# Attention and mixture of experts on one core: the reciprocal of the softmax sums moved in part from VectorE to ScalarE, and the masked scores kept in PSUM

## The chip, the cores and the metric

The kernel runs on 1 core of one Trainium2 chip. The metric is the device time of one execution in microseconds (us), lower is better. The engines are PE (TensorE, matmuls), DVE (VectorE), ACT (ScalarE), POOL (GpSimd) and SP (SyncE, DMA issue).

## The reference, cut to what matters

```python
# x: (4, 1024, 256); 16 heads of 64
proj = x @ W_in.T + b_in
q, k = _rope(q, sin, cos), _rope(k, sin, cos)
att = einsum('bhqd,bhkd->bhqk', q, k) / 8
att = where(causal, att, -inf)
att = softmax(att, axis=-1)             # exp(att - max) / sum
y = einsum('bhqk,bhkd->bhqd', att, v)
x = layernorm(x + y.reshape(...) @ W_out.T + b_out)
...
x = layernorm(x + ffn(x))               # 16 experts, the best 3 of each token
```

The change touches the attention alone: the division by the softmax sum, and the masking of the scores from which the row maxima come.

## The kernel before, in words

Attention is worked in 32 steps (`STEPS`): 4 batches times 8 pairs of heads (`PAIRS`), each step on all 1024 tokens. Every engine runs its own instruction stream, written out by hand as a list of events for one turn (`PE_ORDER`, `ACT_ORDER`, `DVE_ORDER`, `POOL_ORDER`, `SP_ORDER`, lines 37 to 47). `turns` walks these lists for `it` from -2 to 32; a `+` behind an event works on the next step, `++` on the one after it, `-` on the one before. An engine never leaves the order of its list, so an instruction that waits holds back all behind it. The streams are tied by semaphores only. `PE_LAST` and `ACT_LAST` (lines 116, 117) stand in for the lists in the last turn.

The events that matter here, with the line where each is made:

- A (PE, L599) fills `a_ps` with scores of queries against keys, one bank for each of the two heads (.0 and .1), in 12 units of up to 512 columns. M (DVE) takes the negated row maximum: a plain reduction where no entry is masked (L921), and where the unit is on the diagonal a fused instruction (L917 and 918) that subtracts the causal mask, writes the result into `masked` (bf16, SBUF), and gives the minimum; the written tile is never read. A of the next unit waits for M of this one (L637), as they share the bank.
- B (PE, L606 and L607) fills `b_ps` with the transposed scores minus the maxima, E (ACT, L798) takes the exponential into `prob`. B of the next unit and head waits for E of this one (L650): B6.1 waits for E5.1, B7.1 for E6.1, B4.1 for E3.1.
- V (PE, L688) multiplies `prob` with the values into `y_ps`; N (ACT, L835) copies `y_ps` to `yT`.
- The sums over the keys are added up in `acc` for one half of the queries by DVE (k, L955 to L960), for the other by POOL (K, L534); D0 and D1 (PE, L698) sum over the partitions with a matrix of ones into `t_ps`.
- d0 and d1 (ACT, L839) copy `t_ps` to `inv`. R0 to R7 (DVE, L966) take the reciprocal of `inv` in place, 128 columns at a time, four for each half; G0 and G1 (DVE, L970) multiply `yT` by it.
- O0 to O3 (PE, L713) project `yT` with W_out into `t_ps`, o0 to o3 (DVE, L980) add that to the rows of `x1b`.
- `t_ps` is one bank that D, O and X (the turning of the maxima, L708) share, so PE waits before each for the one before it (`wait_misc`, L611 to L622): O1, which comes behind D0, waits for `d_taken` from d0.
- r (DVE, L937) and a, l (POOL, L507 and L512), h (ACT, L811) make the rotated queries and keys and their high and low halves for the step after the next; T (POOL, L520) zeroes the masked corner of `prob`; y (ACT, L830), z (DVE, L892) and u (POOL) are the first layer norm, in some turns only; v (ACT, L821) evicts the values.

Around the change the order on PE is `V3 B5.1 B6.0 A5.1+ O1- A6.0+ B6.1 B7.0 X0+ A6.1+ B7.1`, that on ACT is `d0 h2++ E5.1 E6.0 N0 E6.1`. Half a turn before, PE has `D1- V8- V9- V10- V11- B3.1 B4.0 A4+ B4.1 F1++`, and ACT has `d1- h0++ N1- E3.1 E4.0 E4.1`.

Of the kernel before, what the change touches and what calls it, by code (L numbers as in the profile page):

```python
# [7 lines left out]
ALU = mybir.AluOpType  # L8
ACT = mybir.ActivationFunctionType
AX_X = mybir.AxisListType.X  # L10
F32 = mybir.dt.float32
# [20 lines left out]
def parse(text):  # L32

    return [(w.rstrip("+-"), w.count("+") - w.count("-")) for w in text.split()]
# [5 lines left out]
A10.1+ A11.0+ F3++ A11.1+""")  # L40
ACT_ORDER = parse("""E0.0 E0.1 E1.0 E1.1 E2.0 w1 E2.1 E3.0 d1- h0++ N1- E3.1 E4.0 E4.1 y0 h1++ E5.0 d0 h2++ E5.1 E6.0 N0 E6.1 y1 E7.0
w0+ E8.0 E7.1 h3++ E8.1 y2 E9.0 E9.1 y3 E10.0 v2++ E10.1 E11.0 E11.1 v3++""")
DVE_ORDER = parse("""M11.1 M0.0+ C0 M0.1+ M1.0+ M1.1+ M2.0+ k0 M2.1+ M3.0+ k1 k2 r0++ M3.1+ R4- r1++ R5- M4.1+ k3 M4.0+ R6- R7-
M5.0+ r2++ G1- r3++ z0 M5.1+ o1- M6.0+ R0 M6.1+ R1 M7.0+ R2 R3 G0 z1 M7.1+ o2- M8.0+ M8.1+ M9.0+ o3- M9.1+ M10.0+
o0 M10.1+ M11.0+""")
# [70 lines left out]
PE_LAST = [(e, -1) for e in "V8 V9 V10 V11 t0 D1 t1 g0 O1 g1 O2 l0 O3".split()]  # L116
ACT_LAST = [(e, -1) for e in "N1 c0 d1 c1 e0 f0".split()]
GATED = 4
# [15 lines left out]
def attention_phase(nc, A, dram, shared):  # L134
# [4 lines left out]
    with ExitStack() as ctx:  # L139
# [3 lines left out]
        def sem(name):  # L143
# [18 lines left out]
        acc = sb("acc", [P, 2, 2, 512], F32)  # L162
        inv = sb("inv", [P, 2, 512], F32)
        cos = sb("cos_sb", [P, T], F32)
        sin = sb("sin_sb", [P, T], F32)
        yT = sb("yT", [P, 2, 512], F32)
        ident, bout = shared["ident"], shared["bout"]
        causal = sb("causal", [P, 512], F32)
        masked = sb("masked", [P, 2, 512], BF16)
        ones = sb("ones64", [P, 64], F32)  # L170
# [16 lines left out]
                 "p_fill pv_done y_taken max_all turned d_fill d_taken o_fill o_done rope_read v_taken "  # L187
                 "diag_full cut added hi_done lo_done sum_d sum_p inv_all g_done x_st x_back "
                 "bout_sum bout_all biased ln_stat ln_chain ln_ready normed ln_mean "
# [12 lines left out]
        exp_done = [sem(f"exp_done{h}") for h in range(2)]  # L202
        inv_done = [sem(f"inv_done{c}") for c in range(2)]
        m_row = [sem(f"m_row{c}") for c in range(2)]
# [544 lines left out]
        def _(act):  # L749
# [11 lines left out]
            def finish_high_halves():  # L761
                high_halves(EARLY, NW + NX)
                for i, (r, c) in enumerate(WO_UNITS):
# [3 lines left out]
                                         ACT.Copy).then_inc(m["wo_ev"], 1)  # L767

            high_halves(0, EARLY)

            def turn(it, phase, order):
                for e, ahead in order:
# [59 lines left out]
                    elif kind == "N":  # L832
                        act.wait_ge(m["pv_done"], UNITS * n + (4 if q == 0 else UNITS))
                        wait_for(act, m["o_fill"], 4 * (n - 1) + 2 * q + 2, n - 1)
                        nc.scalar.activation(yT[:, q, :], y_ps[:], ACT.Copy).then_inc(m["y_taken"], 1)  # L835
                    elif kind == "d":
                        act.wait_ge(m["d_fill"], 2 * n + q + 1)
                        wait_for(act, m["g_done"], 2 * (n - 1) + q + 1, n - 1)
                        nc.scalar.activation(inv[:, q, :], t_ps[:], ACT.Copy).then_inc(m["d_taken"], 1)  # L839
                    elif kind == "c":  # L840
                        act.wait_ge(m["x_turned"], q + 1)
                        act.wait_ge(m["added"], 4 * STEPS)
                        nc.scalar.activation(rot[:, q, :], g_ps[:, q, :], ACT.Copy).then_inc(m["x_taken"], 1)
                    elif kind == "e":
                        act.wait_ge(m["lt_fill"], 2)
                        act.wait_ge(m["rope_read"], 4 * STEPS)
                        nc.scalar.activation(cos[0:E_, 0:512], a_ps[0:E_, 0, :], ACT.Copy).then_inc(m["lt_taken"], 1)
                    elif kind == "f":
                        act.wait_ge(m["lt_turned"], 1)
                        nc.scalar.activation(shared["early_lg"][:].rearrange("p t e -> p (t e)"), a_ps[:, 1, 0:GATED * E_],  # L850
                                             ACT.Copy).then_inc(shared["early_in"], 1)
# [4 lines left out]
        def _(dve):  # L856
# [42 lines left out]
            def turn(it, phase, order):  # L899
                for e, ahead in order:  # L900
# [10 lines left out]
                    elif kind == "M":  # L911
# [4 lines left out]
                        if diagonal:  # L916
                            nc.vector.tensor_tensor_reduce(  # L917
                                masked[:, h, 0:w], a_ps[:, h, 0:w], causal[:, 512 - w:512], -1.0, -MASKED, ALU.add,
                                ALU.min, out).then_inc(a_max[h], 1)
# [42 lines left out]
                    elif kind == "R":  # L962
                        c, i = q // 4, q % 4
                        dve.wait_ge(m["d_taken"], 2 * n + c + 1)
                        part = inv[:, c, i * P:(i + 1) * P]
                        nc.vector.reciprocal(part, part).then_inc(inv_done[c], 1)  # L966
                    elif kind == "G":
                        dve.wait_ge(inv_done[q], 4 * (n + 1))
                        dve.wait_ge(m["y_taken"], 2 * n + q + 1)
                        nc.vector.tensor_tensor(yT[:, q, :], yT[:, q, :], inv[:, q, :], ALU.mult)\  # L970
                            .then_inc(m["g_done"], 1)
                    elif kind == "o":
# [6 lines left out]
                        rows = x1[:, first:first + 2, :].rearrange("p t d -> p (t d)")  # L979
                        nc.vector.tensor_tensor(rows, t_ps[:], rows, ALU.add).then_inc(m["o_done"], 1)  # L980

# [859 lines left out]
```

## Time and profile before

| | us |
|---|---|
| three timed runs | 1835.0, 1840.57, 1841.21 |
| median | 1840.57 |
| span of the profiled execution | 1831.6 |

The profiled execution has no time of its own beside its span in what is shown; the span runs from the first to the last instruction, and the median of the timed runs is 9.0 us above it. The attention fills the span from about 90 to 1280 us, then come routing, the experts and the last layer norm. In the views below a row of the timeline gives the start, the length, the engine, the line, the instruction and its tiles, and in brackets the idle time of that engine before it with what ended it. PEld is the loading of weights into PE, which runs ahead of the matmuls.

### The profile page before, as it was taken

The numbers are of one execution on the slowest core, as the hardware profiler recorded it, in microseconds if no ns is written. First come the engines' busy times: TensorE is split into PE (matmuls) and PEld (weight loads), VectorE is DVE, ScalarE is ACT, GpSimd is POOL, SyncE is SP. The second block draws the span as 40 slices with busy tenths as digits, with TensorE's granted clock in tenths as the row PEclk, the third lists the DMA queues.
The fourth block names the chain that finished last, engine by engine and source line by source line (L and its number), as shares of the span: only waits on it lengthen the run. The fifth ranks groups of instructions, "written<-read, shape, count | busy, mean of one in ns | idle before, by whom it ended". The sixth has DMA issues, their size and how long they took to land. (4 is left out here: it accounts for less than half of the span.)

```text
span 1831.6 us, 34098 instructions
## 1 busy us (share of the span) xinstructions
PE 1689.9 (92%) x9515; PEld 1265.2 (69%) x9516; DVE 1381.3 (75%) x3236; ACT 728.9 (40%) x1551; POOL 1233.2 (67%) x1064
## 2 busy tenths in 40 slices
PE   4699999999999999999999999998659999999990
PEld 4566667666766677666766676664249999999980
DVE  3578888888888888988888898885775566556654
ACT  2244444444444544444444444543352222222222
POOL 2266787677877776788777777764017777777764
PEclk8699999999999999999999999999759999999995
DMA  9975566655755776556776564531954444444448
GB/s 310 336 217 151 162 170 201 171 173 157 190 150 177 229 219 190 157 164 199 211 218 187 173 185 139 162 104 50 369 158 72 73 74 72 71 73 74 71 65 278
DMA packets 185571, 302.37 MB, mean 165 GB/s; under 512 B 23632, under 2 KB 82896, under 8 KB 185312
## 3 DMA queue, kind: packets, MB, share of 16 engines
q1 hardware_dynamic: 161872, 269.20, 49.5%
q0 software_dynamic: 21504, 30.29, 10.4%
q10 hardware_dynamic: 2064, 1.31, 0.3%
q8 instruction: 60, 0.98, 0.2%
q14 instruction: 71, 0.58, 0.1%
HBM read 188.81 MB, written 111.67 MB: 164 GB/s over the span
## 5 line engine op out<-in xcount | busy, mean ns | idle before, releaser
L798 ACT ACTIVATE prob<-b_ps 128x512 f32<-128x512 f32 (+3 forms) x768 | 354.4, 488 | 357.0 <-PE b_ps L607 255.8
L534 POOL TENSOR_TENSOR acc<-acc,prob 128x1024 f32<-128x1024 f32 (+1 forms) x192 | 353.0, 1839 | 6.4 <-POOL acc L534 3.7
L606 PE MATMUL b_ps<-q,k 128*128 128x512 f32 (+3 forms) x768 | 295.8, 389 | 4.8 <-ACT prob L798 3.5
L507 POOL TENSOR_TENSOR roped<-rot 128x512 f32<-128x512 f32 x128 | 174.7, 1365 | 164.1 <-DVE rot L937 163.1
L599 PE MATMUL a_ps<-k,q 128*128 128x512 f32 (+3 forms) x768 | 266.2, 383 | 16.9 <-DMA k<-scratch_hilo 6.7
L688 PE MATMUL y_ps<-prob,v_sb 128*64 128x512 f32 (+3 forms) x1536 | 272.9, 490 | 0.1
L917 DVE CUSTOM_DVE_ANT_0 masked<-a_ps,causal 128x128 bf16<-128x128 f32 (+3 forms) x512 | 237.2, 478 | 42.7 <-PE a_ps L599 35.2
L607 PE MATMUL b_ps<-q,k 65*128 65x512 f32 (+3 forms) x768 | 264.2, 348 | 0.0
L1487 POOL DMA_INDIRECT scratch_sum<-y,dst_i x112 | 186.5, 1665 | 96.2 <-ACT y L1559 90.4
L966 DVE RECIPROCAL inv<-inv 128x128 f32<-128x128 f32 x256 | 232.2, 929 | 7.7 <-ACT inv L839 5.3
L512 POOL TENSOR_TENSOR lo<-roped,hi 128x512 fp32r<-128x512 f32 x128 | 177.0, 1383 | 81.2 <-ACT hi L811 81.2
L688 PEld LDWEIGHTS y_ps<-prob,v_sb 128*64 128x64 f32 x1536 | 104.3, 137 | 179.1 <-issue 174.3
L1513 PEld LDWEIGHTS h_ps<-mxT,w_now 128*128 128x128 f32 x1792 | 219.4, 193 | 5.7
L1513 PE MATMUL h_ps<-mxT,w_now 128*128 128x128 f32 x1792 | 219.8, 276 | 0.0
L1522 PE MATMUL yo_ps<-w,hT 128*128 x896 | 211.8, 379 | 0.0
L591 PE MATMUL g_ps<-xT,w_sb 128*128 128x512 f32 x768 | 194.0, 403 | 7.4 <-DVE rot L937 4.5
L921 DVE TENSOR_REDUCE max_b<-a_ps 128x1 f32<-128x512 f32 x256 | 171.7, 672 | 36.2 <-PE a_ps L599 33.1
L606 PEld LDWEIGHTS b_ps<-q,k 128*128 128x128 f32 x768 | 145.0, 189 | 73.9 <-issue 42.1
L599 PEld LDWEIGHTS a_ps<-k,q 128*128 128x128 f32 x768 | 142.8, 191 | 61.9 <-DVE max_b L921 12.8
L1472 POOL DMA_INDIRECT xin<-scratch_xn,src_i x112 | 111.5, 996 | 109.1 <-POOLq L1007 75.3
L591 PEld LDWEIGHTS g_ps<-xT,w_sb 128*128 128x128 f32 x768 | 148.0, 196 | 39.5 <-DVE rot L937 5.5
L1522 PEld LDWEIGHTS yo_ps<-w,hT 128*128 128x128 f32 x896 | 161.6, 190 | 17.4
(258 smaller groups left out, 2393.6 us busy)
## 6 DMA issues: line engine op xcount, KB each, us to landing
q<-scratch_hilo SPq DMA_DIRECT2D x192, 256.0 KB, 4.6
k<-scratch_hilo SPq DMA_DIRECT2D x192, 256.0 KB, 5.2
scratch_hilo<-hi SPq DMA_DIRECT2D x64, 512.0 KB, 4.0
scratch_hilo<-lo SPq DMA_DIRECT2D x64, 512.0 KB, 4.7
w_sb<-scratch_wsplit SPq DMA_DIRECT2D x32, 512.0 KB, 3.7
w<-in_L_ffn_W_dram SPq DMA_DIRECT2D x32, 512.0 KB, 10.1
wv_sb<-scratch_wsplit SPq DMA_DIRECT2D x16, 512.0 KB, 6.2
xT<-scratch_xsplit SPq DMA_DIRECT2D x6, 1024.0 KB, 6.6
```

What stands on the lines that cost most here:

```text
L534: nc.gpsimd.tensor_tensor(sums, old, probs(q), ALU.add).then_inc(m["sum_p"], 1)
L591: ins = nc.tensor.matmul(out, left, right, start=(a, b, k) == PRODUCTS[0], stop=(a, b, k) == PRODUCTS[-1], skip_group_check=True)
L599: nc.tensor.matmul(out, q1[s][:, h, blk * P:(blk + 1) * P], k1[s][:, h, k0:k0 + w], start=True, stop=True, skip_group_check=True).then_inc ...
L606: nc.tensor.matmul(out, k1[s][:, h, js], q1[s][:, h, qs], start=True, stop=False, skip_group_check=True)
L607: ins = nc.tensor.matmul(out, k2[s][0:65, h, js], q2[s][0:65, half, h, 512 - w:512], start=False, stop=True, skip_group_check=True)
L688: ins = nc.tensor.matmul(y_ps[64 * h:64 * h + 64, 512 - w:512], v_sb[:, pairs, j, s, 64 * h:64 * h + 64], probs(q)[:, h, :], start=(j == 0 ...
L798: nc.scalar.activation(probs(q)[:, h, :], b_ps[:, h, 0:w], ACT.Exp).then_inc(exp_done[h], 1)
L917: nc.vector.tensor_tensor_reduce(masked[:, h, 0:w], a_ps[:, h, 0:w], causal[:, 512 - w:512], -1.0, -MASKED, ALU.add, ALU.min, out).then_in ...
L966: nc.vector.reciprocal(part, part).then_inc(inv_done[c], 1)
L1487: pool.indirect_dma_start(out=dram[f"sum{t % SUMS}"], out_offset=bass.IndirectOffsetOnAxis(ap=dst_i[:, t:t + 1], axis=0), in_=y[:, t % 2, ...
L1513: ins = nc.tensor.matmul(h_ps[:, s, c * P:(c + 1) * P], w1_now[:, s, k, c * P:(c + 1) * P], xT[:, s, k * P:(k + 1) * P], start=(k == 0), s ...
L1522: ins = nc.tensor.matmul(yo_ps[:, s, 0:D], hT[:, s, c * P:(c + 1) * P], w2[:, bass.ds(e, 1), c, :].rearrange("p a d -> p (a d)"), start=(c ...
```

## The change

For each half of the queries, ACT now takes three steps where it took one: it copies the sums to a new tile `total`, writes their natural logarithm into `inv`, and, in a new event x, replaces `inv` by exp(-inv), a first guess g of 1/s. DVE makes it exact by one Newton step with the sign turned: `total` becomes s*g, and `inv` becomes (s*g - 2)*g. The two instructions are R0 and R1 for half 0, R2 and R3 for half 1, each over 512 columns; the eight reciprocals are gone. As the result is negated, o now subtracts `t_ps` from the rows. Before the attention a table set of ACT that has both functions is loaded by name. The masked scores are written back to `a_ps` in f32 instead of to `masked` in bf16, and that tile is gone.

```diff
--- before.py
+++ after.py
@@ -38,10 +38,10 @@
 V11- B3.1 B4.0 A4+ B4.1 F1++ A5.0+ B5.0 V0 V1 V2 D0 V3 B5.1 B6.0 A5.1+ O1- A6.0+ B6.1 B7.0 X0+ A6.1+ B7.1
 A7.0+ B8.0 V4 V5 V6 V7 B8.1 A7.1+ B9.0 O2- B9.1 B10.0 A8.0+ F2++ A8.1+ B10.1 A9.0+ O3- B11 A9.1+ A10.0+ O0
 A10.1+ A11.0+ F3++ A11.1+""")
-ACT_ORDER = parse("""E0.0 E0.1 E1.0 E1.1 E2.0 w1 E2.1 E3.0 d1- h0++ N1- E3.1 E4.0 E4.1 y0 h1++ E5.0 d0 h2++ E5.1 E6.0 N0 E6.1 y1 E7.0
+ACT_ORDER = parse("""E0.0 E0.1 E1.0 E1.1 E2.0 w1 E2.1 E3.0 d1- h0++ x1- N1- E3.1 E4.0 E4.1 y0 h1++ E5.0 d0 h2++ x0 E5.1 E6.0 N0 E6.1 y1 E7.0
 w0+ E8.0 E7.1 h3++ E8.1 y2 E9.0 E9.1 y3 E10.0 v2++ E10.1 E11.0 E11.1 v3++""")
-DVE_ORDER = parse("""M11.1 M0.0+ C0 M0.1+ M1.0+ M1.1+ M2.0+ k0 M2.1+ M3.0+ k1 k2 r0++ M3.1+ R4- r1++ R5- M4.1+ k3 M4.0+ R6- R7-
-M5.0+ r2++ G1- r3++ z0 M5.1+ o1- M6.0+ R0 M6.1+ R1 M7.0+ R2 R3 G0 z1 M7.1+ o2- M8.0+ M8.1+ M9.0+ o3- M9.1+ M10.0+
+DVE_ORDER = parse("""M11.1 M0.0+ C0 M0.1+ M1.0+ M1.1+ M2.0+ k0 M2.1+ M3.0+ k1 k2 r0++ M3.1+ r1++ R2- M4.1+ k3 M4.0+ R3-
+M5.0+ r2++ G1- r3++ z0 M5.1+ o1- M6.0+ M6.1+ R0 M7.0+ R1 G0 z1 M7.1+ o2- M8.0+ M8.1+ M9.0+ o3- M9.1+ M10.0+
 o0 M10.1+ M11.0+""")
 POOL_ORDER = parse("""K11- u0 T0 u1 T1 u2 T2 u3 a0++ l0++ T3 a1++ l1++ p0 a2++ l2++ K5 a3++ K6 l3++ K7 T8 T9 K8 T10 K9 T11 K10""")
 SP_ORDER = parse("""L1+ S3+ L0++ W0++ S0++ W1++ S1++ S2++""")
@@ -114,7 +114,7 @@
 ZEROS_FROM, ZERO_PIECES = 12, 11
 ZERO_TILES = (TILES + 1) // ZERO_PIECES
 PE_LAST = [(e, -1) for e in "V8 V9 V10 V11 t0 D1 t1 g0 O1 g1 O2 l0 O3".split()]
-ACT_LAST = [(e, -1) for e in "N1 c0 d1 c1 e0 f0".split()]
+ACT_LAST = [(e, -1) for e in "N1 c0 d1 x1 c1 e0 f0".split()]
 GATED = 4
 
 
@@ -161,12 +161,12 @@
         prob = sb("prob", [P, P_SIZE], F32)
         acc = sb("acc", [P, 2, 2, 512], F32)
         inv = sb("inv", [P, 2, 512], F32)
+        total = sb("total", [P, 512], F32)
         cos = sb("cos_sb", [P, T], F32)
         sin = sb("sin_sb", [P, T], F32)
         yT = sb("yT", [P, 2, 512], F32)
         ident, bout = shared["ident"], shared["bout"]
         causal = sb("causal", [P, 512], F32)
-        masked = sb("masked", [P, 2, 512], BF16)
         ones = sb("ones64", [P, 64], F32)
         bias = sb("bias", [P, 3, PAIRS], F32)
         max_a = sb("max_a", [P, 2, 2, 4], F32)
@@ -185,7 +185,8 @@
 
         names = ("vo_done zeroed wv_ld wsp consts ones_row w_in wv_in tab_in bias_in wo_in setup_tr setup_hi setup_lo wo_ev "
                  "p_fill pv_done y_taken max_all turned d_fill d_taken o_fill o_done rope_read v_taken "
-                 "diag_full cut added hi_done lo_done sum_d sum_p inv_all g_done x_st x_back "
+                 "diag_full cut added hi_done lo_done sum_d sum_p g_done x_st x_back "
+                 "guessed scaled refined "
                  "bout_sum bout_all biased ln_stat ln_chain ln_ready normed ln_mean "
                  "x_turned x_taken lt_fill lt_taken lt_turned").split()
         m = {k: sem(k) for k in names}
@@ -200,7 +201,6 @@
         a_max = [sem(f"a_max{h}") for h in range(2)]
         b_fill = [sem(f"b_fill{h}") for h in range(2)]
         exp_done = [sem(f"exp_done{h}") for h in range(2)]
-        inv_done = [sem(f"inv_done{c}") for c in range(2)]
         m_row = [sem(f"m_row{c}") for c in range(2)]
         m_ld = [sem(f"m_ld{c}") for c in range(2)]
 
@@ -766,6 +766,7 @@
                                          setup_bank(NW + NX + i).rearrange("p (j c) -> p j c", j=4),
                                          ACT.Copy).then_inc(m["wo_ev"], 1)
 
+            nc.scalar.preload_act_table_set("natural_log_exp_and_others")
             high_halves(0, EARLY)
 
             def turn(it, phase, order):
@@ -836,7 +837,13 @@
                     elif kind == "d":
                         act.wait_ge(m["d_fill"], 2 * n + q + 1)
                         wait_for(act, m["g_done"], 2 * (n - 1) + q + 1, n - 1)
-                        nc.scalar.activation(inv[:, q, :], t_ps[:], ACT.Copy).then_inc(m["d_taken"], 1)
+                        wait_for(act, m["refined"], 2 * n + q, 2 * n + q - 1)
+                        nc.scalar.activation(total[:], t_ps[:], ACT.Copy)
+                        nc.scalar.activation(inv[:, q, :], t_ps[:], ACT.Ln).then_inc(m["d_taken"], 1)
+                    elif kind == "x":
+
+                        act.wait_ge(m["d_taken"], 2 * n + q + 1)
+                        nc.scalar.activation(inv[:, q, :], inv[:, q, :], ACT.Exp, scale=-1.0).then_inc(m["guessed"], 1)
                     elif kind == "c":
                         act.wait_ge(m["x_turned"], q + 1)
                         act.wait_ge(m["added"], 4 * STEPS)
@@ -915,7 +922,7 @@
                         out = max_a[:, s, h, blk:blk + 1] if blk < 4 else max_b[:, s, k0 // 512, h, blk - 4:blk - 3]
                         if diagonal:
                             nc.vector.tensor_tensor_reduce(
-                                masked[:, h, 0:w], a_ps[:, h, 0:w], causal[:, 512 - w:512], -1.0, -MASKED, ALU.add,
+                                a_ps[:, h, 0:w], a_ps[:, h, 0:w], causal[:, 512 - w:512], -1.0, -MASKED, ALU.add,
                                 ALU.min, out).then_inc(a_max[h], 1)
                         else:
                             nc.vector.tensor_reduce(out, a_ps[:, h, 0:w], AX_X, ALU.max, negate=True)\
@@ -960,12 +967,17 @@
                             ins = nc.vector.tensor_tensor(sums, sums, probs(q), ALU.add)
                         ins.then_inc(m["sum_d"], 1)
                     elif kind == "R":
-                        c, i = q // 4, q % 4
-                        dve.wait_ge(m["d_taken"], 2 * n + c + 1)
-                        part = inv[:, c, i * P:(i + 1) * P]
-                        nc.vector.reciprocal(part, part).then_inc(inv_done[c], 1)
+                        c = q // 2
+                        if q % 2 == 0:
+                            dve.wait_ge(m["guessed"], 2 * n + c + 1)
+                            nc.vector.tensor_tensor(total[:], total[:], inv[:, c, :], ALU.mult)\
+                                .then_inc(m["scaled"], 1)
+                        else:
+                            dve.wait_ge(m["scaled"], 2 * n + c + 1)
+                            nc.vector.scalar_tensor_tensor(out=inv[:, c, :], in0=total[:], scalar=-2.0, in1=inv[:, c, :],
+                                                           op0=ALU.add, op1=ALU.mult).then_inc(m["refined"], 1)
                     elif kind == "G":
-                        dve.wait_ge(inv_done[q], 4 * (n + 1))
+                        dve.wait_ge(m["refined"], 2 * n + q + 1)
                         dve.wait_ge(m["y_taken"], 2 * n + q + 1)
                         nc.vector.tensor_tensor(yT[:, q, :], yT[:, q, :], inv[:, q, :], ALU.mult)\
                             .then_inc(m["g_done"], 1)
@@ -977,7 +989,7 @@
                             dve.wait_ge(m["biased"], 4 * (n // PAIRS) + q + 1)
                         first = n // PAIRS % 2 * TB + 2 * q
                         rows = x1[:, first:first + 2, :].rearrange("p t d -> p (t d)")
-                        nc.vector.tensor_tensor(rows, t_ps[:], rows, ALU.add).then_inc(m["o_done"], 1)
+                        nc.vector.tensor_tensor(rows, rows, t_ps[:], ALU.subtract).then_inc(m["o_done"], 1)
 
             low_halves(0, EARLY)
             dve.wait_ge(m["tab_in"], 32)
```

## Rows read from the trace of the kernel before

**Rows 1.** The page: the span, and the busy time of each engine over it.
```profile
span 1831.6 us, 34098 instructions
PE 1689.9 (92%) x9515; PEld 1265.2 (69%) x9516; DVE 1381.3 (75%) x3236; ACT 728.9 (40%) x1551; POOL 1233.2 (67%) x1064
```

**Rows 2.** Busy time by engine between two copies d1, one step apart.
```profile
288.65:325.32 36.67, 36.67 (x196) 25.57 (x194) 31.64 (x68) 17.12 (x37) 28.65 (x24) 1.00 0.72 222
```

**Rows 3.** Timeline of ACT: d1 and d0 of one turn, then two d1 in a row.
```profile
288.65 0.60 ACT L839 ACTIVATE inv<-t_ps 128x512 f32<-128x512 f32 x1 [1.03 <-PE t_ps L698]
...
298.88 0.60 ACT L839 ACTIVATE inv<-t_ps 128x512 f32<-128x512 f32 x1 [1.29 <-PE t_ps L698]
...
472.19 0.60 ACT L839 ACTIVATE inv<-t_ps 128x512 f32<-128x512 f32 x1 [1.03 <-PE t_ps L698]
...
509.17 0.60 ACT L839 ACTIVATE inv<-t_ps 128x512 f32<-128x512 f32 x1 [1.03 <-PE t_ps L698]
```

**Rows 4.** Timeline of ACT behind d0: h2, E5.1 and E6.1.
```profile
299.46 0.63 ACT L811 ACTIVATE hi<-roped 128x512 fp32r<-128x512 f32 x1
300.00 0.58 ACT L798 ACTIVATE prob<-b_ps 128x512 f32<-128x512 f32 x1
...
301.90 0.60 ACT L798 ACTIVATE prob<-b_ps 128x512 f32<-128x512 f32 x1
```

**Rows 5.** Timeline of PEld: the weights of B6.1 and of B7.1.
```profile
301.00 0.19 PEld L606 LDWEIGHTS b_ps<-q,k 128*128 128x128 f32 x1
...
302.55 0.19 PEld L606 LDWEIGHTS b_ps<-q,k 128*128 128x128 f32 x1 [0.19 <-ACT prob L798]
```

**Rows 6.** Timeline of ACT behind d1 (h0, N1, E3.1), and weights of B4.1.
```profile
289.98 0.63 ACT L811 ACTIVATE hi<-roped 128x512 fp32r<-128x512 f32 x1 [0.73 <-POOL roped L507]
290.81 0.60 ACT L835 ACTIVATE yT<-y_ps 128x512 f32<-128x512 f32 x1 [0.20 <-PE y_ps L688]
291.30 0.27 ACT L798 ACTIVATE prob<-b_ps 128x128 f32<-128x128 f32 x1
...
291.71 0.19 PEld L606 LDWEIGHTS b_ps<-q,k 128*128 128x128 f32 x1
```

**Rows 7.** Groups by line and form: busy us, mean ns of one, idle time before.
```profile
L966 DVE RECIPROCAL inv<-inv 128x128 f32<-128x128 f32 x256 | 232.2, 929 | 7.7 <-ACT inv L839 5.3
L811 ACT ACTIVATE hi<-roped 128x512 fp32r<-128x512 f32 x128 | 80.8, 631 | 93.1 <-POOL roped L507 91.1
L980 DVE TENSOR_TENSOR x1b<-t_ps,x1b 128x512 f32<-128x512 f32 x128 | 88.4, 691 | 42.0 <-PE t_ps L713 34.0
L917 DVE CUSTOM_DVE_ANT_0 masked<-a_ps,causal 128x512 bf16<-128x512 f32 x128 | 87.6, 685 | 8.8 <-PE a_ps L599 8.8
L960 DVE TENSOR_TENSOR acc<-acc,prob 128x512 f32<-128x512 f32 x32 | 22.1, 692 | 18.0 <-POOL prob L520 17.9
```

**Rows 8.** Timeline: DVE's G0, and the POOL instruction that runs when it starts.
```profile
306.74 1.23 DVE L970 TENSOR_TENSOR yT<-yT,inv 128x512 f32<-128x512 f32 x1
305.05 2.37 POOL L534 TENSOR_TENSOR acc<-acc,prob 128x1024 f32<-128x1024 f32 x1
```

**Rows 9.** Waits of PEld, 215.29 to 435.39 us (six steps): total us, times, longest.
```profile
PEld t_ps L713 <- DVE x1b L980: 1.8, 6, 0.3
...
PEld b_ps L606 <- ACT prob L798: 1.2, 6, 0.2
PEld a_ps L599 <- DVE max_a L917: 1.0, 6, 0.2
PEld a_ps L599 <- DVE max_b L921: 0.9, 6, 0.2
```

**Rows 10.** Timeline of DVE and PE after the last d1: reciprocals, then O2.
```profile
1271.41 3.39 DVE L966 RECIPROCAL inv<-inv 128x128 f32<-128x128 f32 x4 [5.34 <-ACT inv L839]
1276.18 1.13 PE L713 MATMUL t_ps<-woT,yT 128*128 128x256 f32 x4 [1.85 <-DVE x1b L980]
```

**Rows 11.** Groups by line: ACT's table load, the only one before the combine.
```profile
L759 ACT ACT_TABLE_LOAD x1 | 1.3, 1283 | 0.6 <-PEq L1828 0.6
```

## Prediction

> **What bounds the kernel now.** I read the page first, and it shows PE busy for 92% of the span, DVE for 75%, ACT for only 40% [rows 1]. By these shares the change takes work from an engine that is nearly full and gives it to one that is more than half idle. The share is an average, so I then cut out one step. From one copy d1 to the next, 325.32 - 288.65 = 36.67 us, PE is busy for the whole 36.67 us at a granted clock of 1.00, DVE for 31.64 us and ACT for 17.12 us [rows 2]. PE sets the step; anything that holds PE back once is lost for good, and DVE's work counts only where PE waits for it. So the third view is what PE's weight loading waits for: in six steps 1.8 us for o (rows of `x1b`), 1.0 and 0.9 us for M, and 1.2 us for E [rows 9]. That is 0.62 us of a step for DVE and 0.20 us for ACT. The 0.20 us is one place: the weights of B7.1 are loaded at 302.55, 0.05 us after E6.1 ends (301.90 + 0.60) [rows 4, 5]. ACT, idle for half of the step, is late at that place already. The last view is the timeline there, since the new instructions of ACT stand just ahead of it.
>
> **The reciprocals on DVE.** Removed: 8 a step of 929 ns, 7.43 us [rows 7]. Added: R0 to R3, each with two inputs of 512 columns from SBUF, nearest to the 692 ns of the add on `acc` [rows 7]: 2.77 us. DVE is relieved of 4.66 us a step, some 149 us over 32 steps. What of it is on the path? The reciprocals stand beside V4 to V7 and F1 of PE's order, matmuls that need nothing of DVE. The 0.62 us that PE waits for DVE is at O0 and at A, where DVE has itself just waited for PE: a round trip and not a backlog. I count nothing for the plain steps. In the steps with statistics of the layer norm DVE is fuller: one of them takes 509.17 - 472.19 = 36.98 us, 0.31 more than the plain one [rows 3]. There are two in each of three batches, the other less clear; between 0 and 6 x 0.31 = 1.9 us, I take **-1.2 us**. At the end of the attention the last four reciprocals lie bare: 3.39 us on DVE, and O2 waits for G1 behind them [rows 10]. In their place come a logarithm (0.5), an exponential (0.6) and two DVE instructions (2 x 0.6, as neighbours overlap by some 0.08), 2.3 us: **-1.1 us**.
>
> **The logarithm and the exponential on ACT, behind d0.** Now ACT has d0 at 298.88, h2 at 299.46, E5.1 at 300.00 to 300.58 [rows 3, 4]. Then the stream is d0, Ln, h2, x0, E5.1. What one instruction adds is its pitch and not its length. From a start to the next the rows give 0.58 us (d0 to h2) and 0.54 us (h2 to E5.1); N1 to E3.1 gives 0.49 [rows 3, 4, 6]. Ln reads PSUM as N1 and E3.1 do, so 0.50; x0 reads and writes SBUF like h (631 ns [rows 7]), so 0.57. E5.1 starts and ends 1.07 us later, at 301.65. B6.1 must wait for that, and its weights are loaded at 301.00 [rows 5]; with the same 0.05 us that moves to 301.70. So 0.35 us of slack is used up and **PE stands still for 0.70 us**. All behind B6.1 keeps its distance: E6.1 can't start before B6.1 has ended, B7.1 not before E6.1, so the 0.20 us wait stays and doesn't absorb it. Ln also delays `d_taken`, for which O1 waits: about 0.1 us, hidden in the 0.70 us. The wait of d0 for `refined` costs nothing, as in DVE's order that R3 has M5.0, r2 and G1 behind it by then; h2's wait for POOL stays, its input being there. POOL's l2, behind h2, comes 0.5 us later, covered by POOL's idle time of 36.67 - 28.65 = 8.0 us a step [rows 2]; without that cover it would push K5 and through it E9.0. 30 full steps x 0.70 = 21.0 us, and the last two turns, without h2, lose 0.6 each: **+22.2 us**.
>
> **The same behind d1.** Copy and Ln fit between 288.65 and h0 at 289.98 [rows 3, 6], which waits for POOL. x1 follows h0: N1 starts not at 290.81 but at 289.98 + 0.57 + 0.54 = 291.09, E3.1 at 291.58 for 291.30, and ends at 291.85. The weights of B4.1, at 291.71 now, come at 291.90 [rows 6]: 0.19 us x 30 = **+5.7 us**. If x1 ran 0.1 us faster this would halve, so its ends are 0 and +8 us.
>
> **The new waits on DVE.** R0 to R3 have two inputs in SBUF, and such an instruction doesn't run beside POOL's. G0 starts at 306.74, takes 1.23 us where it needs about 0.68, and ends 0.55 us after POOL's add, which ended at 307.42 [rows 8]; a single-input reciprocal shows no such stretching (929 ns in the mean of 256 [rows 7]). Each R may thus stand for up to POOL's 2.37 us and hold M, r and G behind it. R2 and R3 make r2, r3 and with them o1 and X0 some 0.3 us late, which the 0.70 us of PE's standstill covers; R0, R1 and G0 stand ahead of M7.1, for which A8.1 waits; but V4 to V7, B8.1, A7.1, B9, B10.0, O2, A8.0 and F2 lie between on PE, so that it takes several full stalls in a row to be late. I take 0, with ends 0 and +12 us (0.4 us a step).
>
> **The masked scores in PSUM.** The trace has no DVE instruction that writes PSUM. The nearest rows compare reads: an add with one input in PSUM takes 691 ns, one with both in SBUF 692 [rows 7], so the place of an operand costs nothing, and the masked 512 columns at 685 ns show no extra to be saved either. ACT's 631 against 600 ns makes 35 ns the upper bound. Six of these instructions a step lie in a chain with A: 0 to 6 x 0.035 x 31 = 6.5 us, and 0 below. I take **0**, by the nearer row. The Trainium skill (VectorE: DVE Perf Modes, the section on the errata of TRN2) gives 58 fixed cycles for SBUF to SBUF and 120 for PSUM to SBUF; were the store dearer by that difference, about 65 ns, an estimate from that page would be +12 us instead of 0. The two adds above show no such difference for the read side, and no run here yet shows the store.
>
> The subtraction in o costs what the addition did. The load of the named table set takes the place of the one at the start (1283 ns [rows 11]), when ACT has nothing to do yet.
>
> **Sum.** -1.2 - 1.1 + 22.2 + 5.7 + 0 + 0 = +25.6 us, on a span of 1831.6 us: 1857 us. The median of the runs is 9 us above that span, so I forecast 1840.6 + 25.6 = **1866 us**, slower by 1.4%. Its own range, from the ends above, is 1855 to 1880.
>
> **The rivals.**
> Faster: the waits for DVE are backlog after all. If all 0.62 us a step went [rows 9], with the -2.3 us above and ACT's additions hidden, it would be 1840.6 - 18.6 - 2.3 = 1820 us. It decides if E5.1 ends less than 0.35 us later, that is, if x0 and Ln together cost under 0.35 us. Against it: each takes 0.5 or more in every row of ACT. 0.10.
> No change: PE's standstill gives the other engines 0.70 us, and the waits of 0.62 us later in the step shrink by nearly as much; with the reciprocals gone they might. 25.6 - 18.6 leaves +7, 1848 us. Against it: those waits follow matmuls of PE by a fixed time. 0.08.
> Much slower by port: R0 and R1 each stand behind a full POOL add, M7.1 misses A8.1 by about 1 us a step: 1866 + 30 = 1896 us. For it G0's row [rows 8], against it all that PE has ahead of A8.1. 0.10.
> The change doesn't do what it says: if the exponentials and logarithms didn't stay in one table set, four loads a step at 1283 ns [rows 11], most of them where ACT is on the path, would give 1866 + 32 x 4 x 1.28 = 2030 us. The Trainium skill (ScalarE: Activation LUTs, the section on table sets) says that one set holds both and that two sets would cost a load at each switch; the trace shows one load for Copy and Exp together and can't show Ln. 0.03.
> The forecast keeps 0.69.
>
> **How the numbers follow.** A measurement of this kernel can tell about 0.5%, 9 us. Slower is the forecast and the last two rivals, 0.69 + 0.10 + 0.03 = 0.82; same 0.08; faster 0.10. The range of 8 in 10 takes the forecast's own, stretched a little to both sides toward the second and third rivals: 1850 to 1885.
>
> **What the profile after would show.** Right: the step is 37.5 to 37.6 us; the weights of B6.1 wait 0.7 us for E5.1; a Ln of about 600 ns and an Exp of about 630; no RECIPROCAL of 128 columns, and DVE busy some 150 us less; the masked group still at 685 ns. Wrong: a step near 36.7 us, B6.1 without a wait, or four R that add their stalls to M and A instead.

## The result and the profile after

The changed kernel takes 1875.38 us (median of 4 runs, 1868.4 to 1877.72) against 1838.87 us of the kernel before on the same chip: a ratio of 1.0199, 95% interval 1.0178 to 1.0221. It is 36.5 us slower; the forecast was 25.6 us slower, with 1866 us in a range of 1850 to 1885. The profiled execution is the fastest of the four, by 5.6 us and more, and has the highest mean clock, 0.963 for 0.958 to 0.959; what is read from its trace is that of the best case.

The page of the changed kernel, first lines of it, to set beside [rows 1]:

```profile
span 1866.7 us, 34099 instructions
PE 1704.4 (91%) x9515; PEld 1257.8 (67%) x9516; DVE 1399.3 (75%) x3108; ACT 778.8 (42%) x1679; POOL 1291.9 (69%) x1064
```

DVE isn't less busy, as it was to be by 149 us, but busier by 18. The groups say why (columns as in [rows 7]):

```profile
L924 DVE CUSTOM_DVE_ANT_0 a_ps<-a_ps,causal 128x512 f32<-128x512 f32 x128 | 89.9, 702 | 8.0 <-PE a_ps L599 8.0
L973 DVE TENSOR_TENSOR total<-total,inv 128x512 f32<-128x512 f32 x64 | 71.7, 1120 | 7.2 <-ACT inv L846 7.1
L977 DVE SCALAR_TENSOR_TENSOR inv<-total,inv 128x512 f32<-128x512 f32 x64 | 69.5, 1086 | 0.1
L982 DVE TENSOR_TENSOR yT<-yT,inv 128x512 f32<-128x512 f32 x64 | 121.7, 1902 | 1.2
L924 DVE DVE_READ_ACCUMULATOR2_ANT max_a<- 128x1 f32 x256 | 35.9, 140 | 0.0
L935 DVE TENSOR_TENSOR max_c<-max_b 128x8 f32<-128x8 f32 x32 | 26.6, 830 | 0.1
L846 ACT ACTIVATE inv<-inv 128x512 f32<-128x512 f32 x64 | 39.9, 623 | 0.2
L842 ACT ACTIVATE inv<-t_ps 128x512 f32<-128x512 f32 x64 | 37.9, 592 | 0.0
```

The four new instructions of a step take 1120 and 1086 ns where 692 was reckoned, and G, which the change doesn't touch, 1902 ns where it took 967. All of them have two inputs in SBUF, like the G0 of [rows 8] that stood behind POOL's add. So has C0, the minimum over 16 numbers a partition: 830 ns for 310. The read of the accumulator behind a masked unit takes 140 ns for 82.

A plain step between two copies d1, by the windows view, to set beside [rows 2]:

```profile
296.76:334.63 37.87, 37.35 (x196) 25.32 (x194) 32.66 (x64) 18.54 (x40) 30.55 (x24) 1.00 0.70 212
```

It has grown from 36.67 to 37.87 us, by 1.20 us; PE, busy for 37.35 us of it, now stands still for 0.52 us. The timeline of ACT shows d1, d0 with what stands behind it, and the next d1:

```profile
296.76 0.60 ACT L841 ACTIVATE total<-t_ps 128x512 f32<-128x512 f32 x1 [1.03 <-PE t_ps L698]
...
307.05 0.60 ACT L841 ACTIVATE total<-t_ps 128x512 f32<-128x512 f32 x1 [1.29 <-PE t_ps L698]
307.54 0.59 ACT L842 ACTIVATE inv<-t_ps 128x512 f32<-128x512 f32 x1
308.02 0.63 ACT L812 ACTIVATE hi<-roped 128x512 fp32r<-128x512 f32 x1
308.54 0.63 ACT L846 ACTIVATE inv<-inv 128x512 f32<-128x512 f32 x1
309.06 1.09 ACT L799 ACTIVATE prob<-b_ps 128x512 f32<-128x512 f32 x2
...
334.63 0.60 ACT L841 ACTIVATE total<-t_ps 128x512 f32<-128x512 f32 x1 [1.03 <-PE t_ps L698]
```

And the weights of B6.1, B7.0 and B7.1, to set beside B6.1 and B7.1 of [rows 5]:

```profile
309.71 0.19 PEld L606 LDWEIGHTS b_ps<-q,k 128*128 128x128 f32 x1 [0.57 <-ACT prob L799]
...
310.20 0.19 PEld L606 LDWEIGHTS b_ps<-q,k 128*128 128x128 f32 x1 [0.19 <-ACT prob L799]
...
311.17 0.19 PEld L606 LDWEIGHTS b_ps<-q,k 128*128 128x128 f32 x1 [0.21 <-ACT prob L799]
```

From d1 to d0 it is 10.29 us for 10.23, from d0 to B7.1 4.12 us for 3.67. That leaves 1.20 - 0.06 - 0.45 = 0.69 us for the rest of the step, where ACT has nothing new. It is here (timeline of DVE, POOL and PEld):

```profile
326.80 0.97 DVE L935 TENSOR_TENSOR max_c<-max_b 128x8 f32<-128x8 f32 x1
327.69 0.29 DVE L924 CUSTOM_DVE_ANT_0 a_ps<-a_ps,causal 128x128 f32<-128x128 f32 x1
...
326.45 1.29 POOL L534 TENSOR_TENSOR acc<-acc,prob 128x512 f32<-128x512 f32 x1
...
328.09 0.19 PEld L599 LDWEIGHTS a_ps<-k,q 128*128 128x128 f32 x1 [0.68 <-DVE max_a L924]
```

C0 starts while POOL adds (326.45 to 327.74) and ends at 327.77. M0.1 stands behind it, and the weights of A1.1 wait 0.68 us for M0.1. In the kernel before, POOL's add is nearly over when C0 starts, and C0 is short:

```profile
318.14 0.21 DVE L928 TENSOR_TENSOR max_c<-max_b 128x8 f32<-128x8 f32 x1
317.03 1.30 POOL L534 TENSOR_TENSOR acc<-acc,prob 128x512 f32<-128x512 f32 x1
```

So 0.94 us of POOL's add lie behind the start of C0 now, and 0.19 us before. The waits of the weight loading in six steps of the changed kernel, 220.94 to 448.57 us, beside [rows 9]:

```profile
PEld b_ps L606 <- ACT prob L799: 5.8, 18, 0.6
PEld a_ps L599 <- DVE max_a L924: 5.4, 12, 0.7
...
PEld t_ps L713 <- DVE x1b L992: 1.8, 6, 0.3
```

ACT's share has grown from 1.2 to 5.8 us, that of `max_a` by nearly as much, from 1.0 to 5.4; o has stayed.

### The profile page after: what moved, and what is told of

Same layout as the page of the kernel before. It is cut to its first block and busy times, and to the rows that moved or that the text cites. A ratio compares the mean times of both kernels' runs of the same rounds, so it can differ in the third digit from the quotient of the medians.

```text
span 1866.7 us, 34099 instructions
## 1 busy us (share of the span) xinstructions
PE 1704.4 (91%) x9515; PEld 1257.8 (67%) x9516; DVE 1399.3 (75%) x3108; ACT 778.8 (42%) x1679; POOL 1291.9 (69%) x1064
## 5 line engine op out<-in xcount | busy, mean ns | idle before, releaser
L534 POOL TENSOR_TENSOR acc<-acc,prob 128x1024 f32<-128x1024 f32 (+1 forms) x192 | 365.6, 1904 | 6.4 <-POOL acc L534 6.4
L599 PE MATMUL a_ps<-k,q 128*128 128x512 f32 (+3 forms) x768 | 271.6, 387 | 25.5 <-DVE max_a L924 9.4
L507 POOL TENSOR_TENSOR roped<-rot 128x512 f32<-128x512 f32 x128 | 189.1, 1477 | 132.9 <-DVE rot L944 132.2
L924 DVE CUSTOM_DVE_ANT_0 a_ps<-a_ps,causal 128x128 f32<-128x128 f32 (+3 forms) x512 | 248.1, 499 | 32.8 <-PE a_ps L599 26.5
L512 POOL TENSOR_TENSOR lo<-roped,hi 128x512 fp32r<-128x512 f32 x128 | 193.0, 1508 | 98.4 <-ACT hi L812 98.4
L520 POOL TENSOR_SCALAR_AFFINE_SELECT prob<-prob 128x256 f32<-128x256 f32 x256 | 124.8, 493 | 79.4 <-ACT prob L799 58.4
```

The source lines that it names most:

```text
L507: nc.gpsimd.tensor_tensor(roped[:], rot[:, 0, :], rot[:, 1, :], ALU.subtract if half else ALU.add).then_inc(m["added"], 1)
L512: nc.gpsimd.tensor_tensor(lo[:, half, cs], roped[:], hi[:, half, cs].bitcast(F32), ALU.subtract).then_inc(m["lo_done"], 1)
L534: nc.gpsimd.tensor_tensor(sums, old, probs(q), ALU.add).then_inc(m["sum_p"], 1)
L599: nc.tensor.matmul(out, q1[s][:, h, blk * P:(blk + 1) * P], k1[s][:, h, k0:k0 + w], start=True, stop=True, skip_group_check=True).then_inc ...
L924: nc.vector.tensor_tensor_reduce(a_ps[:, h, 0:w], a_ps[:, h, 0:w], causal[:, 512 - w:512], -1.0, -MASKED, ALU.add, ALU.min, out).then_inc( ...
```

## The experiments

Theory after the result: a plain step pays three prices, ACT's delay of B6.1 (together with the part behind d1 0.06 + 0.45 = 0.51 us), C0 standing behind POOL, and the store in PSUM. Rivals: only one of the latter two is real, or ACT isn't on the path. Each ratio is to the kernel before on the same chip; the runs were made on different chips, so they are set beside each other by their ratios. A step is the distance of two d1, in turns without layer norm if nothing else is said. The edits are cut to the lines that matter.

**The store alone.** The kernel before with

```diff
-                                masked[:, h, 0:w], a_ps[:, h, 0:w], causal[:, 512 - w:512], -1.0, -MASKED, ALU.add,
+                                a_ps[:, h, 0:w], a_ps[:, h, 0:w], causal[:, 512 - w:512], -1.0, -MASKED, ALU.add,
```

> The kernel before, with the masked scores written back to a_ps in f32; nothing else. In the profile of the change the read of the accumulator behind each masked unit takes 140 ns where it took 82, and the masked instruction 702 for 685 ns (512 columns). Theory: the store in PSUM costs this much and no more, so with POOL undisturbed the plain step goes from 36.67 to 36.8 to 37.0 us, and the run is 3 to 10 us slower than before. Rival: the store alone makes the 0.68 us that the stretch from V4 to the next D1 has grown, and the run is 20 us slower or more.

Measured: 1839.61 us, 1.0020 (1.0008 to 1.0031). The step by the windows view:

```profile
291.04:327.91 36.87, 36.87 (x196) 25.59 (x194) 32.20 (x68) 17.14 (x37) 28.69 (x25) 1.00 0.72 220
```

The read of the accumulator, by groups:

```profile
L916 DVE DVE_READ_ACCUMULATOR2_ANT max_a<- 128x1 f32 x256 | 36.1, 141 | 0.0
```

The step is 0.20 us longer, as expected, and the run by its ratio 3.7 us slower (1.5 to 5.7 by the interval). The rival, 20 us or more, is out.

**The changed kernel with the store in SBUF.**

```diff
+        masked = sb("masked", [P, 2, 512], BF16)
-        mrow = [sb(f"mrow{c}", [8, P], F32R) for c in range(2)]
+        mrow = [k2[c][96:104, 0, 0:P] for c in range(2)]
-                                a_ps[:, h, 0:w], a_ps[:, h, 0:w], causal[:, 512 - w:512], -1.0, -MASKED, ALU.add,
+                                masked[:, h, 0:w], a_ps[:, h, 0:w], causal[:, 512 - w:512], -1.0, -MASKED, ALU.add,
```

> The changed kernel with the masked scores written to a bf16 tile in SBUF as before (to make room, the two 8-row tiles of the maxima lie in unused rows 96 to 103 of k2). Theory: the accumulator read goes back to 82 ns, but C0 still stands behind an add of POOL, so the run is only 3 to 10 us faster than the changed kernel, 1.014 to 1.018 of before, with a plain step of 37.6 to 37.8 us. Rival (the store makes the 0.68 us): about 1.008 of before, with a step of 37.2 us.

Measured: 1874.09 us, 1.0200 (1.0176 to 1.0223), no gain. The step falls only by 0.07 us:

```profile
301.95:339.75 37.80, 37.24 (x196) 25.32 (x194) 32.30 (x64) 18.85 (x40) 30.41 (x24) 1.00 0.71 214
```

The rival (37.2 us) is out, and the ratio lies outside what the theory gave too. The timeline of this run shows why so little came back:

```profile
331.95 1.05 DVE L936 TENSOR_TENSOR max_c<-max_b 128x8 f32<-128x8 f32 x1
331.69 1.28 POOL L535 TENSOR_TENSOR acc<-acc,prob 128x512 f32<-128x512 f32 x1
```

C0 again ends 0.03 us behind POOL's add, so what DVE has saved ahead of it, C0 waits longer. The prices of the store and of C0 don't simply add up: with C0 held by POOL, the store's 0.20 us is worth 0.07.

**C0 with one input.**

```diff
-                        nc.vector.tensor_tensor(max_c[:, s], max_b[:, s, 0], max_b[:, s, 1], ALU.min)\
+                        nc.vector.tensor_reduce(max_c[:, s], max_b[:, s].rearrange("p k h i -> p h i k"), AX_X, ALU.min)\
```

> The changed kernel with C0 (the minimum of the two halves of max_b, 16 numbers a partition) as a reduction with one input instead of an operation with two inputs in SBUF. In the profile of the change it takes 830 ns for 310 before, 970 in the plain step, as it stands behind POOL's add. Theory: with one input it doesn't stand behind POOL; it takes under 0.3 us, the 0.68 us wait of the weights of A1.1 goes down to 0.1, and the step falls by 0.4 to 0.6 us to about 37.4: 12 to 19 us faster than the change, 1.009 to 1.013 of before. Rival: C0 isn't on PE's path, step and time stay at 37.9 us and 1.02.

Measured: 1866.33 us, 1.0169 (1.0148 to 1.0190). The group of C0:

```profile
L935 DVE TENSOR_REDUCE max_c<-max_b 128x8 f32<-128x16 f32 x32 | 5.5, 171 | 0.1
```

The windows view of the step:

```profile
333.64:371.01 37.37, 37.22 (x196) 25.36 (x194) 31.39 (x64) 18.55 (x40) 29.39 (x23) 1.00 0.61 171
```

The step does what was expected, 0.50 to 0.53 us less, and the theory on C0 holds. The time doesn't: the ratios differ by 0.0030, that is 5.5 us, and their intervals overlap, instead of the 12 to 19 us expected. In the two profiles, first d1 to last, it is 1158.09 us for 1163.84, 5.75 us less. What is missing there lies in the three turns in which POOL computes the roots of the layer norm, which are longer by 1.4 to 1.7 us each, 4.7 in all, and in the five turns behind them, which gain nothing. One of the three, 520.87 to 562.31, takes 41.44 us, where the changed kernel has 39.75 (and the kernel before 38.09). In it, by the timeline of PE:

```profile
526.58 0.47 PE L606 MATMUL b_ps<-q,k 128*128 128x512 f32 x1 [2.05 <-ACT prob L799]
...
527.12 4.50 PE L591 MATMUL g_ps<-xT,w_sb 128*128 128x512 f32 x12
```

And two stretches of the windows view, whose eighth number is the granted clock:

```profile
524.50:527.10 2.60, 0.55 (x3) 0.49 (x3) 2.39 (x3) 2.29 (x5) 1.79 (x3) 1.00 0.00 0
527.10:531.50 4.40, 4.40 (x14) 3.43 (x13) 3.12 (x5) 1.23 (x2) 3.60 (x4) 0.61 0.01 4
```

PE stood still for 2.05 us, and then the clock was granted at 0.61 in the mean of the next 4.4 us, that is, for most of it at the lower of its two levels (1.2 GHz): the 12 matmuls of F1 take 4.50 us. In the changed kernel the timeline of PE at the same place reads:

```profile
529.80 0.47 PE L606 MATMUL b_ps<-q,k 128*128 128x512 f32 x1 [1.63 <-ACT prob L799]
...
530.35 2.91 PE L591 MATMUL g_ps<-xT,w_sb 128*128 128x512 f32 x12
```

And its windows view of F1:

```profile
530.30:533.30 3.00, 3.00 (x15) 2.46 (x15) 3.00 (x5) 1.23 (x2) 2.19 (x3) 1.00 0.00 0
```

Full clock behind 1.63 us. But the length of the standstill doesn't decide it. The third turn of this kind in the changed kernel keeps the full clock behind 2.02 us:

```profile
1140.95 0.47 PE L606 MATMUL b_ps<-q,k 128*128 128x512 f32 x1 [2.02 <-ACT prob L799]
...
1141.50 2.90 PE L591 MATMUL g_ps<-xT,w_sb 128*128 128x512 f32 x12
```

And the second one of the run without Newton step, further down, has the lower clock behind 1.26 us:

```profile
823.85 0.47 PE L606 MATMUL b_ps<-q,k 128*128 128x512 f32 x1 [1.26 <-ACT prob L799]
...
824.39 4.50 PE L591 MATMUL g_ps<-xT,w_sb 128*128 128x512 f32 x12
```

In the run with the store in SBUF two of the three such turns have it (1.80 and 2.12 us, 41.4 and 41.7 us long) and one hasn't (1.76 us, 39.8 us long). So the profile of the run with C0's repair differs from that of the changed kernel by the clock in all three turns, by 1.6 us in the one above. That the repair brings this about isn't shown: each kernel has one profile, and that of the changed kernel is the fastest of its executions. What is shown is that PE's wait there became longer, from 1.63, 1.65 and 2.02 us to 2.05 or 2.06; in the first two turns most of the half microsecond gained ahead of it is lost in waiting.

**No logarithm and no exponential.** R still reads two inputs in SBUF, at the same place.

```diff
-                        nc.scalar.activation(total[:], t_ps[:], ACT.Copy)
-                        nc.scalar.activation(inv[:, q, :], t_ps[:], ACT.Ln).then_inc(m["d_taken"], 1)
+                        nc.scalar.activation(total[:], t_ps[:], ACT.Copy).then_inc(m["d_taken"], 1)
-                        nc.scalar.activation(inv[:, q, :], inv[:, q, :], ACT.Exp, scale=-1.0).then_inc(m["guessed"], 1)
+                        nc.scalar.sem_inc(m["guessed"], 1)
-                            nc.vector.tensor_tensor(total[:], total[:], inv[:, c, :], ALU.mult)\
+                            nc.vector.tensor_tensor(total[:], total[:], causal[:], ALU.max)\
```

> The changed kernel without the logarithm and the exponential on ACT (d only copies the sums, x only signals), and with R reading total and causal from SBUF and taking a maximum in place of the product, so that the values stay finite: the same instructions and ports on DVE, no Newton step. Theory: the delays of B6.1 and B7.1 (0.46 us a step) and of the first half (0.06) go, while R's stalls beside POOL stay; the step is 37.4 us if C0 still stands behind POOL and down to 36.9 if POOL, no longer late behind h2, has finished by then: 1.003 to 1.012 of before. Rival: ACT isn't what holds PE, and the run stays at 1.018 or more.

Measured: 1858.42 us, 1.0124 (1.0104 to 1.0145). A step, by the windows view:

```profile
371.27:408.64 37.37, 37.04 (x196) 25.53 (x194) 31.96 (x64) 17.00 (x37) 29.31 (x23) 1.00 0.61 169
```

ACT's two instructions are worth 0.50 to 0.53 us a step; C0 still takes 914 ns here, so its stall doesn't come from h2 and l2 being late. The plain turns are of two kinds in this run: the early ones take 37.68 us and A1.1 waits 0.97 us in them instead of 0.65, for the same M behind C0.

**No Newton step.**

```diff
-M3.1+ r1++ R2- M4.1+ k3 M4.0+ R3-
+M3.1+ r1++ M4.1+ k3 M4.0+
-M6.1+ R0 M7.0+ R1 G0
+M6.1+ M7.0+ G0
-                        dve.wait_ge(m["refined"], 2 * n + q + 1)
+                        dve.wait_ge(m["guessed"], 2 * n + q + 1)
-                        nc.vector.tensor_tensor(rows, rows, t_ps[:], ALU.subtract).then_inc(m["o_done"], 1)
+                        nc.vector.tensor_tensor(rows, rows, t_ps[:], ALU.add).then_inc(m["o_done"], 1)
```

> The changed kernel without R0 to R3: G multiplies by the first guess exp(-ln s) itself, o adds again; the copy, the logarithm, the exponential on ACT and the store in PSUM stay as they are. Left out is the Newton step that makes the guess exact. Theory (the three prices add up: ACT 0.52 us a step, C0 beside POOL 0.53, the store 0.20): without R POOL isn't late, C0 takes 0.3 us again, and the plain step is 36.67 + 0.52 + 0.20 = 37.4 us; 1.009 to 1.013 of before. Rival (C0's stall comes from h2 and l2 being late behind the logarithm): the step stays at 37.9 us, 1.018 or more.

Measured: 1854.04 us, 1.0102 (1.0085 to 1.0119). The group of C0:

```profile
L934 DVE TENSOR_TENSOR max_c<-max_b 128x8 f32<-128x8 f32 x32 | 7.9, 248 | 0.1
```

The windows view of the step:

```profile
292.87:330.27 37.40, 37.25 (x196) 25.36 (x194) 26.64 (x60) 18.55 (x40) 28.67 (x24) 1.00 0.72 219
```

37.40 us, the value that the prices of ACT and the store gave without that of C0. POOL's busy time is back from 30.55 to 28.67 us, and its add ends 0.04 us behind the start of C0 instead of 0.94. So the stall of C0 is R's doing: with R there, POOL is late, and its add reaches into C0. The 1.88 us of busy time say that POOL's own instructions are stretched beside R and G; how much of the lateness comes from that, and how much from DVE's handing over later, wasn't separated.

**C0 alone, in the kernel before.** The edit of C0 above.

> The kernel before with only C0 as a reduction with one input. Theory: C0 takes 170 ns for 310 and had slack there, so the time is the same, 0.997 to 1.001 of before. Rival: C0 was on PE's path before already, the step falls by 0.14 us and more, 0.996 or less.

Measured: 1834.58 us, 0.9997 (0.9986 to 1.0007). C0 cost nothing before; its price is one of the change.

**A version against both.** On top of the edits without Newton step, with C0 as above and `masked` in SBUF:

```diff
-d1- h0++ x1- N1- E3.1 E4.0 E4.1 y0 h1++ E5.0 d0 h2++ x0 E5.1
+d1- h0++ N1- E3.1 E4.0 E4.1 y0 h1++ x1- E5.0 d0 h2++ E5.1
-w0+ E8.0 E7.1 h3++ E8.1
+w0+ E8.0 E7.1 h3++ x0 E8.1
-                        nc.scalar.activation(total[:], t_ps[:], ACT.Copy)
                         nc.scalar.activation(inv[:, q, :], t_ps[:], ACT.Ln).then_inc(m["d_taken"], 1)
```

> A version meant to beat both: d writes the logarithm of the sums straight from t_ps in place of the copy (no instruction more), the exponential stands where ACT is idle (x1 behind h1, x0 behind h3), no reciprocal and no Newton step (so the factor has the accuracy of the tables), C0 with one input, the masked scores in SBUF. DVE has 7.4 us a step less than before, ACT 1.2 us more in idle time. Theory (PE sets the step, DVE's relief is worth nothing in a plain step): the step stays at 36.67 us and the gain is that of the steps with layer norm and of the end, 2 to 6 us: 0.996 to 1.000 of before. Rival (the waits for DVE are backlog): down to 36.1 us a step, 0.99.

Measured: 1831.9 us, 0.9976 (0.9962 to 0.9991). A step, by the windows view:

```profile
255.25:291.94 36.69, 36.69 (x196) 25.58 (x194) 25.91 (x60) 17.93 (x39) 28.62 (x24) 1.00 0.56 159
```

DVE is busy for 25.91 us of it where it was 31.64, and the step is the same 36.7 us. This is what the relief of DVE is worth: nothing in a plain turn, and 3.1 us in all by the medians (4.4 by the ratio, 1.7 to 7.0 by the interval). It beats both kernels, the one before by a quarter of a percent, at the price of a factor that has no Newton step to correct it; how much less exact it is wasn't measured.

**Everything kept, but placed elsewhere.** All the arithmetic of the change, two tiles of `total` (with `mrow` in `k2` as above), C0 with one input, the store in PSUM.

```diff
-d1- h0++ x1- N1- E3.1 E4.0 E4.1 y0 h1++ E5.0 d0 h2++ x0 E5.1
+d1- h0++ N1- E3.1 E4.0 E4.1 y0 n1- h1++ x1- E5.0 d0 h2++ E5.1
-w0+ E8.0 E7.1 h3++ E8.1
+w0+ E8.0 E7.1 n0 h3++ x0 E8.1
-M3.1+ r1++ R2- M4.1+ k3 M4.0+ R3-
-M5.0+ r2++ G1- r3++
+M3.1+ r1++ M4.1+ k3 M4.0+
+M5.0+ r2++ R2- R3- G1- r3++
-M6.1+ R0 M7.0+ R1 G0 z1 M7.1+ o2- M8.0+ M8.1+
+M6.1+ M7.0+ R0 z1 M7.1+ R1 o2- M8.0+ G0 M8.1+
+                    elif kind == "n":
+                        nc.scalar.activation(inv[:, q, :], total[:, q, :], ACT.Ln).then_inc(m["guessed"], 1)
```

> The changed kernel, with all of its arithmetic, with the work moved off the places where PE waits: the logarithm is taken from total (two tiles of it now) and stands with the exponential where ACT is idle (behind E4.1 and behind E7.1), R2 and R3 stand behind r2, R0 and R1 around M7.1, C0 has one input; the store in PSUM stays. Theory: ACT's 0.52 us and C0's 0.53 us go, the store's 0.20 stays: a plain step of 36.9 us, 1.002 to 1.008 of before. Rival: the four R stand behind POOL's adds on M's path wherever they are, and the run is at 1.012 or more.

Measured: 1863.6 us, 1.0156 (1.0139 to 1.0173). The plain step is as expected, by the windows view:

```profile
293.70:330.65 36.95, 36.93 (x196) 25.58 (x194) 30.01 (x64) 19.21 (x41) 29.43 (x24) 1.00 0.73 222
```

The time is not; the ratio is where the rival had it, above 1.012, but by other turns than the plain ones that the rival spoke of. In the six turns with statistics of the layer norm a step takes 39.96 to 41.54 us, for instance 41.50 us (441.59 to 483.09). The timeline in it, rows of DVE, of POOL and of PE:

```profile
462.11 2.74 DVE L978 SCALAR_TENSOR_TENSOR inv<-total,inv 128x512 f32<-128x512 f32 x1
...
465.97 2.37 DVE L983 TENSOR_TENSOR yT<-yT,inv 128x512 f32<-128x512 f32 x1
...
461.91 2.38 POOL L534 TENSOR_TENSOR acc<-acc,prob 128x1024 f32<-128x1024 f32 x1
...
465.44 2.35 POOL L534 TENSOR_TENSOR acc<-acc,prob 128x1024 f32<-128x1024 f32 x1
...
468.99 1.03 PE L599 MATMUL a_ps<-k,q 128*128 128x384 f32 x2 [1.19 <-DVE max_b L929]
```

R1 and G0 each stand for a whole add of POOL on the path of M, PE waits 1.19 us at A9, and the clock falls behind it (0.65 in the mean of 472 to 475 us). So where R1 and G0 stand later, a stall of the kind of the forecast's third rival appears, at A9 and not at A8.1, and only in the turns where the statistics fill DVE as well.

## Why the prediction was right, and where its sizes were off

- **PE sets the step and a delay in it is lost: right.** 36.67 us plus 0.20 (store, measured alone), 0.51 (ACT: 0.06 before d0 and 0.45 behind) and 0.50 to 0.53 (C0) is 37.88 to 37.91 us; most plain turns measure 37.86 to 37.97. The sums fit the steps of all runs but one: with the store in SBUF 37.7 would be due, and 37.80 was measured, as C0 took up what the store gave back.
- **ACT behind d0: the right mechanism, 0.70 us forecast, 0.45 measured.** E5.1 starts 309.06 - 307.05 = 2.01 us behind d0 for 1.12, later by 0.89 and not by 1.07. The stream has four pitches now, 0.49, 0.48, 0.52 and 0.52 us, where it had two, 0.58 and 0.54. I had left the old two as they were and added 0.50 and 0.57; but the pitches of h2's neighbours changed too. The rest of the difference is that B7.0 and B7.1 made up 0.09 us of B6.1's delay, where I had let nothing make up.
- **ACT behind d1: 0.19 us forecast, 0.06 measured.** The weights of B4.1 do come 0.19 us later, 3.25 us behind d1 (300.01 - 296.76) for 3.06. What I had wrong is that this is lost for good: the loads behind them make up 0.13 us, and 0.06 is left at d0.
- **Nothing from DVE's relief in a plain turn: right**, shown by the version without R and reciprocals, with 5.7 us less of DVE and the same step. The 149 us less of busy time were wrong: the term "four instructions of 692 ns" should have been 1120 and 1086, and G went from 967 to 1902 ns. In the turns with layer norm I took 1.2 us off for those with statistics; they grew by 0.96 to 1.26 us where a plain one grew by 1.20, which makes 0.65. The others I had left out: the turns with the roots grew by 1.7 to 2.3 us, the five behind them by only 0.2 to 0.6.
- **The new waits on DVE: this is the step that failed.** I took 0, and looked for the trouble at M7.1 alone. The stalls beside POOL were of the kind that [rows 8] show, but they cost where I hadn't looked: they make POOL late, and another instruction with two inputs in SBUF, C0, then runs into POOL's add right ahead of M0.1, for which A1.1 waits. It costs 0.50 to 0.53 us a step, beyond my end of 0.4, at another place and by another instruction.
- **The masked scores in PSUM: 0 forecast, 0.20 us a step and by the ratio 3.7 us in all measured**, inside the bounds of 0 to 6.5 us. The price is mostly not in the masked instruction (702 for 685 ns) but in the read of the accumulator behind it (141 for 82 ns), which I hadn't priced. The 65 ns a piece that I had estimated from the Trainium skill (VectorE: DVE Perf Modes, the section on the errata of TRN2) for a store that costs like its PSUM read is nearer to the sum of both, 76 ns, than my 0; that page gives no time for the read of an accumulator or for a store in PSUM, so the nearness explains nothing.
- **The end of the attention: 1.1 us less forecast, 0.8 measured.** In place of 3.39 us of reciprocals there are two instructions of 0.69 us, and O2's matmuls start 4.57 us behind the last d1 for 5.40; they wait 1.03 us for 1.85 [rows 10].
- **The table set held**: Ln and Exp alternate without a load between them, and there is still one load before the combine; I had given the rival 0.03.

The two errors had opposite signs: 0.38 us a step too much for ACT, about 0.7 too little for C0 and the store. The forecast missed the 36.5 us by 11 us, and its range held it; that it missed by no more is in part luck, as the error for ACT hid half of the other. The narrower range of the sum, 1855 to 1880, isn't what its own ends give: added up they give 1860 to 1888.

## What to carry to other kernels

An engine that is idle half of the time can still be the one that is waited for, as ACT is here; before giving it work, find the semaphore that stands behind the new instruction in its queue, and how long its user can wait. And instructions of DVE with two inputs in SBUF stall beside POOL's adds here, and make POOL late in turn: count not only what a new one waits for, but what it makes late on POOL, and which other instruction of this kind then meets POOL at another place. A one-input form took C0 out of that.

## What the runs showed of the hardware that I had not expected

- A minimum over 16 numbers a partition with two SBUF inputs takes 0.97 us when POOL adds at that moment, and in a form with one input 171 ns in the mean of 32, though POOL's add still runs beside it.
- The accumulator read behind the masked minimum takes 82 ns when the result goes to SBUF as bf16, and 140 ns when it goes to PSUM as f32. Which of the two, place or type, makes it wasn't tried.
- At the same place of the program, the 12 matmuls behind a standstill of PE ran at the full clock behind 1.27, 1.63, 1.76 and 2.02 us and for the most part at the lower one behind 1.26, 1.80, 2.05 and 2.12 us: up to 4.50 us for what takes 2.91. The length of the standstill doesn't decide between the two, and what does stays open. It matters for the reading of small gains: three such turns differ by some 5 us in all, as much as the ratios give for C0's repair.
